# Eight sequences without a loop, score units in two halves, and a step order by priorities

## The reference, cut to what matters

```python
x = x + causal_attention(layernorm(x), Wq, Wk, Wv, Wo)      # 16 heads of 16, rotary, causal
x = x + routed(layernorm(x), Wg, Wq, Wk, Wv, Wo)            # half of the tokens by gate, 16 heads of 16
x = x + biased_attention(layernorm(x), w_qkv, w_out, bias)  # 16 heads of 64, relative bias
x = x + routed(layernorm(x), Wg, Wq, Wk, Wv, Wo)
```

## Time and profile before

| | us |
|---|---|
| median of three runs | 2933.91 (2921.36 to 2938.8) |
| profiled execution | 2932.05 |
| its span, first to last instruction | 2930.3 |
| TensorE busy | 2390.6 (82%) |
| VectorE, ScalarE, GpSimd busy | 1303.9, 1131.5, 533.8 |
| DMA | 98.24 MB, 34 GB/s |

### The profile page before, as it was taken

The page is one execution under the profiler, slowest core; times in us unless marked ns, Lnnn a source line. Parts: engine busy times, 40 slices in busy tenths (PEclk is TensorE's granted clock), DMA queues, the critical chain, the costliest instruction groups (busy, mean ns, idle before and its releaser), DMA issues. The chain is left out here.

```text
span 2930.3 us, 38346 instructions
## 1 busy us (share of the span) xinstructions
PE 2390.6 (82%) x15600; PEld 1367.1 (47%) x15616; DVE 1303.9 (44%) x3344; ACT 1131.5 (39%) x1873; POOL 533.8 (18%) x755
## 2 busy tenths in 40 slices
PE   5578888887888888788788878888878888888996
PEld 3344455443455444554345543554435544355554
DVE  3345453453434445444354354544435444354433
ACT  2234442444424344244442434424444234443551
POOL 2102221121201222012220122101221112211220
PEclk8889999999999899999999989999999998999998
DMA  2001110110001110011100101001010010001100
GB/s 97 1 18 43 37 37 19 37 51 24 31 19 37 51 37 31 7 44 44 37 31 11 51 31 37 31 23 41 31 37 31 24 47 28 31 31 42 55 21 8
DMA packets 28919, 98.24 MB, mean 34 GB/s; under 512 B 2752, under 2 KB 11328, under 8 KB 28608
## 3 DMA queue, kind: packets, MB, share of 16 engines
q1 hardware_dynamic: 28736, 95.70, 9.7%
HBM read 91.49 MB, written 4.19 MB: 33 GB/s over the span
## 5 line engine op out<-in xcount | busy, mean ns | idle before, releaser
L641 ACT ACTIVATE probs<-probs,peak 128x512 f32<-128x512 f32 x512 | 365.2, 714 | 608.9 <-DVE peak L819 608.7
L577 POOL TENSOR_SCALAR probs<-probs,rtotal 128x512 f32<-128x512 f32 x512 | 354.6, 706 | 1221.6 <-DVE rtotal L823 1221.6
L813 DVE CUSTOM_DVE_ANT_0 probs<-ps,band 128x512 f32<-128x512 f32 x512 | 332.1, 686 | 397.1 <-PE ps L1057 397.1
L648 ACT ACTIVATE PT<-ps 128x1024 f32<-128x1024 f32 x256 | 259.9, 1016 | 168.4 <-PE ps L1064 167.8
L1057 PE MATMUL ps<-KT,QT 64*128 64x512 f32 x1024 | 299.3, 662 | 10.7 <-ACT PT L648 3.9
L729 DVE TENSOR_REDUCE mcol<-ps 128x4 f32<-128x512 f32 (+3 forms) x128 | 187.8, 1490 | 242.3 <-PE ps L901 242.3
L1064 PE MATMUL ps<-ident,probs 128*128 128x128 f32 x2048 | 279.6, 281 | 7.4 <-ACT PTc L606 3.8
L484 PE MATMUL ps<-xnT,wb 128*128 128x512 f32 x512 | 273.1, 663 | 14.1 <-ACT xnT L593 8.9
L1064 PEld LDWEIGHTS ps<-ident,probs 128*128 128x128 f32 x2048 | 235.0, 144 | 90.6 <-issue 77.1
L1071 PE MATMUL ps<-PT,Vb 128*64 128x512 f32 x1024 | 254.8, 643 | 3.7 <-ACT PT L648 3.7
L606 ACT ACTIVATE PTc<-ps 128x1536 f32<-128x1536 f32 (+1 forms) x96 | 152.5, 1589 | 147.2 <-PE ps L914 146.8
(11 more groups left out here) (125 smaller groups left out, 3124.4 us busy)
## 6 DMA issues: line engine op xcount, KB each, us to landing
band<-in_band SPq DMA_DIRECT2D x64, 896.0 KB, 4.6
wb<-in_w_b SPq DMA_DIRECT2D x64, 384.0 KB, 3.0
x<-in_x SPq DMA_DIRECT2D x8, 512.0 KB, 4.0
out<-x SPq DMA_DIRECT2D x16, 256.0 KB, 2.2
wob<-in_wo_b SPq DMA_DIRECT2D x1, 1024.0 KB, 7.0
wqk<-in_wqk_a SPq DMA_DIRECT2D x1, 512.0 KB, 4.5
wva<-in_wv_a SPq DMA_DIRECT2D x1, 256.0 KB, 4.1
woa<-in_wo_a SPq DMA_DIRECT2D x1, 256.0 KB, 4.2
```

The source lines that it names most:

```text
L577: last = g.tensor_scalar(unit, unit, rtotal[:, r % 8, e:e + 1], 1.0, ALU.mult, ALU.mult)
L641: last = a.activation(unit, unit, ACT.Exp, bias=peak[:, r % 8, e:e + 1], accum_out=total[:, r % 8, e:e + 1])
L648: a.activation(PT[:, k % 2, :, :, tile_of(q)], bank(now).rearrange("p e (k n) -> p e k n", k=NT), ACT.Copy).then_inc(act_read, 1)
L813: last = v.tensor_tensor_reduce(out=probs[:, r % ROWS_HELD, e, :], in0=bank(now)[:, e, :], in1=band[:, k % 2, e, lo:lo + T], scale=1.0, sc ...
```

## The change

The three lists of steps now name for each step what it needs and what it must follow; `whole` joins the parts of all eight sequences, and `in_order` makes the order. It simulates the engines with the durations of `WORK` (in us; the first entry is where a step begins) and takes, again and again, the step with the smallest `key`: the time at which it could start (inputs, banks, 0.1 us for another tile shape, 0.15 us for a signal), less the allowance of its kind in `EARLY`; no start counts as earlier than TensorE's next free moment. Ties go to the step with the longest chain of needs behind it. A biased part's first steps may come before the last rows of the one before. By the table, the 99 TensorE steps of a biased part add up to 145 us (`b_q` and `b_k` 1.75, `b_v` 1.85, `b_xt` .95, others below), and the allowances of one sequence's side steps and biased transposes to 96 us.

Each `c_p1`, `c_p2`, `f_p1`, `f_p2` has two units of two banks, `o` for heads 0 and 1 and `o2` for heads 2 and 3, anywhere in PSUM. TensorE waits for room in both, and raises the first unit's signal after the last matmul of head 1. The reader waits and reads twice. `f_p1` and `f_p2` are changed as `c_p1` and `c_p2` are. There is one program for all steps, without loop or barriers between; what was cleared by them counts on (`16 * (k // 2 + 1)` and the like), and waits for the first loads stand where the data is first used.

```diff
 UNITS = {
...
-    "c_p1": [("o", "dve", 4)], "c_m": [("o", "dve", 1)], "c_p2": [("o", "act", 4)], "c_val": [("o", "act", 1)],
+    "c_p1": [("o", "dve", 2), ("o2", "dve", 2)], "c_m": [("o", "dve", 1)],
+    "c_p2": [("o", "act", 2), ("o2", "act", 2)], "c_val": [("o", "act", 1)],
...
-    "f_p1": [("o", "dve", 4)], "f_m": [("o", "dve", 1)], "f_p2": [("o", "act", 4)], "f_val": [("o", "act", 1)],
+    "f_p1": [("o", "dve", 2), ("o2", "dve", 2)], "f_m": [("o", "dve", 1)], "f_p2": [("o", "act", 2), ("o2", "act", 2)],
+    "f_val": [("o", "act", 1)],
...
+WORK = {
+    "c_ln": [("dve", 2.4), ("pool", 1.6), ("dve", 1.8)],
+    "c_xt": [("pe", .95), ("act", 1.1)],
...
+    "f_gate": [("dve", .35)],
+    "f_row": [("pe", .5), ("dve", 3.8)],
+    "f_rank": [("pe", 1.9), ("dve", 3.1)],
+    "f_gather": [("pe", 3.5), ("act", .6)],
...
+    "f_p1": [("pe", .95), ("dve", 1.24), ("dve", 1.24)],
+    "f_m": [("pe", .3), ("dve", .4)],
+    "f_p2": [("pe", .95), ("act", 1.03), ("act", 1.03)],
...
+    "b_row": [("pe", .95), ("dve", 1.75), ("act", 1.85)],
+    "b_nrm": [("dve", .17), ("pool", 1.4)],
+    "b_tr": [("pe", .9), ("act", 1.05)],
+    "b_val": [("pe", 3.55), ("dve", .7)],
+    "b_y": [("pe", 6.95), ("dve", 2.1)],
+    ("c_p1", 0): [("pe", 1.15), ("dve", .97), ("dve", .97)],
...
+TILES = {"c_p2": 1, "f_p1": 1, "f_p2": 1, "b_row": 2, "c_val": 3, "f_val": 3, "b_val": 4}
+CHANGE, SIGNAL = 0.1, 0.15
+
+EARLY = {
+    "b_k": -0.5, "b_ln": 0.25, "b_v": -0.57, "b_xt": 2.17, "b_y": 0.44, "c_ln": 0.15, "c_m": 0.5, "c_ot": 1.06,
+    "c_p1": 0.5, "c_p2": 2.06, "c_qk": 1.11, "c_rot": 0.64, "c_t1": 0.5, "c_turn_k": 0.5, "c_turn_q": 0.5,
+    "c_v": 0.89, "c_val": 0.5, "c_xt": 0.67, "c_y": 0.77, "f_gate": 1.71, "f_gather": 1.51, "f_k": 0.54, "f_ln": 0.69,
+    "f_m": 0.65, "f_o": 0.25, "f_p1": 0.61, "f_p2": 1.25, "f_q": 0.35, "f_rank": 1.28, "f_row": 0.53, "f_t1": 0.53,
+    "f_v": 0.74, "f_val": 0.73, "f_y": 0.65,
 }
...
+STORE_LOAD, FETCH = 6.5, 4.6
...
+    for g in range(4):
         for u in range(3):
...
+            out.append((c("p1", g, u), [c("turn_q", g // 2), c("turn_k", g // 2)],
+                        ([c("m", g - 2)] if g >= 2 else []) + ([c("p1", g, u - 1)] if u else [])))
+            out.append((c("p2", g, u), [c("m", g)],
+                        ([c("val", g - 1, u)] if g else [c("v", 1)]) + ([c("p2", g, u - 1)] if u else [])))
+            out.append((c("val", g, u), [c("p2", g, u), c("v", 1)], [c("val", g, u - 1)] if u else
+                        [c("val", g - 1, 2)] if g else []))
+        out.append((c("m", g), [c("p1", g, 2)], []))
+    for i in range(2):
...
+def whole():
+
+
+    steps = []
+
+    def add(layer, needs, follows):
+        first, a, b = layer[0]
+        steps.extend([(first, a + needs, b + follows)] + layer[1:])
+        return [layer[-1][0]]
+
+    entered = add(causal_steps(0), [], [])
+    side = entered = add(ffn_steps(0, 1), entered, [])
+    for s in range(B):
+        biased = add(biased_steps(s, s - 1 if s else None), entered, [])
+        gone = []
+        if s > 0:
+            side = gone = add(ffn_steps(s - 1, 3), left, side)
+        if s + 1 < B:
+            side = add(causal_steps(s + 1), gone, side)
+            side = entered = add(ffn_steps(s + 1, 1), side, [])
+        left = biased
+    add(ffn_steps(B - 1, 3), left, side)
+    return steps
...
+def in_order(steps):
+
+
+    known = {x for x, _, _ in steps}
+    work = {x: WORK[x.kind if x.kind in WORK else (x.kind, x.q)] for x in known}
+    needs = {x: [(y, SIGNAL + (STORE_LOAD if x.kind == "c_ln" else FETCH if x.kind == y.kind == "b_row" else 0))
...
+    def spot(banks):
+        return min(range(0, BANKS, banks), key=lambda b: (max(bank_free[b:b + banks]), max(bank_used[b:b + banks])))
+
+    while ready:
+        best = None
+        for x in ready:
+            if xn_held and x.kind in ("c_ln", "f_ln", "b_ln"):
+                continue
+            engine = work[x][0][0]
+            start = max([free[engine]] + [done[y] + wait for y, wait in needs[x]])
+            if engine == "pe":
+                if TILES.get(x.kind, 0) != tiles:
+                    start += CHANGE
+                if x.kind != "c_val" or x.q == 0:
+                    units = UNITS[x.kind]
+                    banks = units[0][2]
+                    start = max(start, sorted(max(bank_free[b:b + banks]) for b in range(0, BANKS, banks))[len(units) - 1])
+            key = (max(start, free["pe"] + 0.1) - EARLY.get(x.kind, 0), -chain[x])
+            if best is None or key < best[0]:
+                best = key, x, start
+        _, x, t = best
+        ready.remove(x)
+        emptied = {"act": [], "dve": []}
+        for i, (engine, us) in enumerate(work[x]):
+            t = max(t + (SIGNAL if i else 0), free[engine]) + us
+            free[engine] = t
+            if i and engine != "pool":
+                emptied[engine].append(t)
+        if work[x][0][0] == "pe":
+            tiles = TILES.get(x.kind, 0) if x.kind != "c_p1" else 0
+        done[x] = t
+        for i, (name, reader, banks) in enumerate(UNITS.get(x.kind, ())):
+            opened = x._replace(q=0) if x.kind == "c_val" else x
+            at = banks_of[x, name] = banks_of[opened, name] if opened in done and opened != x else spot(banks)
+            for b in range(at, at + banks):
+                bank_free[b] = emptied[reader][min(i, len(emptied[reader]) - 1)] + SIGNAL
+                if x.kind == "c_val" and x.q < 2:
+                    bank_free[b] = 1e9
+                bank_used[b] = len(order)
+        if x.kind in ("c_ln", "f_ln", "b_ln"):
+            xn_held = True
+        if x.kind in ("c_xt", "b_xt", "f_gather"):
+            xn_held = False
+        order.append(x)
...
-                            pool.wait_ge(act_read, plan.unit(now, now))
+                            pool.wait_ge(act_read, plan.unit(now, now, "o2"))
...
                         if kind == "c_p1":
                             e = n % 2
-                            for t, o, w in c_p1_parts(q):
-                                last = v.tensor_reduce(max_places(mcol[:, e, t, :], e), bank(now)[:, :, o:o + w],
-                                                       AXIS.X, ALU.max)
-                            last.then_inc(dve_read, 1)
+                            for i, name in enumerate(("o", "o2")):
+                                dve.wait_ge(dve_full, plan.unit(now, now, name))
+                                for t, o, w in c_p1_parts(q):
+                                    last = v.tensor_reduce(max_places(mcol[:, e, t, :], e)[:, 2 * i:2 * i + 2],
+                                                           bank(now, name)[:, :, o:o + w], AXIS.X, ALU.max)
+                                last.then_inc(dve_read, 1)
...
                             read(now, Step("c_turn_q", s, l, c))
                             read(now, Step("c_turn_k", s, l, c))
                             room(now)
+                            room(now, "o2")
+                            o = head_banks(now)
                             parts = c_p1_parts(q)
                             for i, (t, at_, w) in enumerate(parts):
                                 for h in range(4):
-                                    te.matmul(o[:, h, at_:at_ + w], Qz[group(h), c, e, tile_of(t)], K1[group(h), c, e, 0:w],
+                                    te.matmul(o[h][:, at_:at_ + w], Qz[group(h), c, e, tile_of(t)], K1[group(h), c, e, 0:w],
                                               start=(i == 0), stop=False)
                             for i, (t, at_, w) in enumerate(parts):
                                 for h in range(4):
-                                    last = te.matmul(o[:, h, at_ + w - P:at_ + w], identb[:], later[:], start=False,
+                                    last = te.matmul(o[h][:, at_ + w - P:at_ + w], identb[:], later[:], start=False,
                                                      stop=(i == len(parts) - 1))
+                                    if i == len(parts) - 1 and h == 1:
+                                        full(last, now)
+                            full(last, now, "o2")
+                            continue
...
-            nc.all_engine_barrier(sems_to_clear=stretch_sems)
...
-        stretch(causal_steps(0), {}, {}, False)
-        with nc.Block() as loaded:
-            @loaded.sync
-            def _(sp):
-                sp.wait_ge(w_rest, 6 * 16)
-                sp.wait_ge(b_first, 5 * 16)
-        stretch(ffn_steps(0, 1), {}, {}, False)
-        stretch(stretches([0], False, True, False), {}, {}, True)
-        with nc.Fori(0, B - 3, 2) as it:
-            stretch(stretches([1, 0], True, True, False), {0: it, 1: it + 1}, {0: it + 2, 1: it + 3}, True)
-        stretch(stretches([1], True, False, True), {0: B - 2, 1: B - 1}, {}, False)
+        layers()
```

More of the change, by code:

```diff
@@ L158 @@
-TURN_LAG = 3
-def biased_steps(s):
-    l = 2
[L164 to L185, removed]
@@ L188, in spread, with c @@
```

(34 more changed lines are left out.)

339 lines of the change are left out of this document (192 added, 147 removed).

## The result

The changed kernel takes 2453.4 us in the median of four runs (2451.0 to 2454.8) against 2929.5 of the kernel before in the same comparison: a ratio of 0.837 (0.834 to 0.840). The profiled span is 2450.3 us.

A forecast was written before the change was run, and what follows sets the result against it. TensorE's time (idle, half clock, work) was taken as the bound. Middle 2107.7 / (1 - 0.095 - 0.028) = 2403, head 173, tail 62, sum 2638, with 1.75 around the span 2640 us (-10%); own range 2540 to 2740, over all 2470 to 2850.

The forecast's parts named there:

- What bounds the kernel: Whole kernel: TensorE's time; in the 2671.2 us middle, 434.5 us idle, 129 us clock cost, 2107.7 us full-clock work.
- (a): No loop or barriers: gaps before norms' transposes and VectorE's waits for x shrink, worth 29 to 60 us.
- (b): Split score units: extra reading hides; causal part alone gains 14 us, the lone routed parts 5 and 4 us.
- (c): New order in the middle, biased steps as filler: 28 us idle of some 315 a sequence, 9.5% against 16.3%.
- The clock: Middle: half-clock cost follows the idle share at a ratio of 0.30, so 9.5% idle brings 2.8%.
- dense stretch: Kernel before, 2680 to 2864 us, little side work mixed in: TensorE 3.8% idle at clock 0.99, taken as a bound.
- the 2107.7 us of work stay: Middle: matmuls keep their number and shape, so full-clock work remains 2107.7 us.
- Dense: Rival, middle: biased steps fill everything, idle 3.8%, clock cost 1.1%, 2453 us in all; chance 0.17.
- The side chain ends last: Rival: routed, causal, routed parts in sequence delay the next biased part; 335 to 358 us a sequence, 2695 to 2833; chance 0.18.
- Little is gained: Rival: readers' delays cause idle time whatever the order; only barriers and x waits go, 2890 us; chance 0.09.
- Allowances used in full: Rival, TensorE's queue before side steps: all 96 us a sequence is waited, 3155 us, slower; chance 0.09.
- Bunched transposes: Rival, biased rows' transposes: 421 ns in place of 273 for 2048, adding 303 us, 2943 us; chance 0.01.

The follow-up runs named there:

- unroll: The kernel before's order and four-bank units, written out for all eight sequences without loop and barriers; 2884.9 us, ratio 0.986 against the kernel before.
- serial: The change, but the next biased part's norm may start only when the last biased part's output is added; 2595.6 us, 0.885 of the kernel before.
- early2: The change with all allowances in `EARLY` doubled; 2694.3 us, 0.918 of the kernel before.
- four_same: The change's very order of steps with four-bank units, only the split undone; 2550.3 us, 0.871 of the kernel before.
- early0: The change with all allowances in `EARLY` set to zero; 2967.1 us, 1.012 of the kernel before.
- early01: The change with all allowances in `EARLY` at a tenth; 2670.1 us, 0.910 of the kernel before.
- order_only: The new order planned for four-bank units, no loop, no split, biased transposes also following the second last b_v; 2596.4 us, 0.887 of the kernel before.
- row_twice: The change with each biased row's two matmuls issued twice into the same banks, same order of steps; 2631.0 us, 0.897 of the kernel before.
- tuned_b: The change with other simulation constants, allowances found anew, biased norm's transposes also behind the second last b_v; 2436.0 us against the change's 2450.8.
- early2b: The change with allowances doubled and each biased norm's transposes also behind the two b_v steps before the last; 2725.4 us, 0.929 of the kernel before.

## Why the prediction was wrong, step by step

**What bounds the kernel** was right: TensorE's time, made of idle time, clock and work, and idle time that an order with biased filler can take away.

**(a)** "Worth 29 at least, 60 at most" held by the number: *unroll* gained 35. Its mechanism held only in part. The waits before norms' transposes fell by 16 us and not by 29, and VectorE's wait for x stayed at 29.1 of 31.2 us. It is the new order that took it away; this is the changed kernel:

```profile
L755 DVE BATCH_NORM_STATS2 stats<-x 128x6 f32<-128x256 f32 x128 | 48.1, 418 | 11.8 <-PEq L1210 10.2
```

What was not priced there is the overlap of two biased parts, which only the new order uses and which *serial* puts at 145 us.

**(b)** Duration and count of the halves were right and hidden. The gain of the parts that run alone was sized too small: causal part 91.4 us (forecast 100), routed 58.4 (60), tail 61 (62): 211 us after the loads where the sum had 222. And the split was priced only for these lone parts. In the middle I let it come under (c); it is worth 100 to 112 us over the kernel. The bank waits that I read were those for other score units; the 45.7 us behind biased units were left out.

**(c)** is the step that failed: "28 us of some 315, and with a little from the biased part itself 9.5% idle" (the terms as listed make 29). It was 18.3 us of 294 (294.33 - 276.02), 6.2%. I took each allowance as a wait that happens. For the score units that was near: second scores waited 3.6 us in the causal part and 4.2 in the routed ones, where 3.6 and 4.8 were counted, and first causal scores 2.8 us for banks, where the count had 4. The others hardly came: the norms' transposes were given 2.8 us a sequence, the first projection 1.1 and the turn-backs 2.1, and none of these waits in the steady period; for row, rank and gather it was 6.6, and 1.9 came. As I read the key, an allowance only bites where the step's input is nearly there and nothing else is; a long reader (3.8 us for the ranks) is bridged by biased rows first. No run tests this reading by itself.

**The clock** was mis-sized too: "a ratio of 0.30" between clock cost and idle share. It was 0.28 before, with the windows in the right place, and here 6.3% idle brought 0.4%, a ratio of 0.06. The dense stretch's 0.99 was a rounded figure for 184 us, and the 0.30 came from an order with 43 gaps of over 2 us (135 us in all); the change has none behind its first transposes.

The middle's miss of 177 us (2403 against 2226) so divides into idle time 228 - 139 = 89, clock 67 - 8 = 59, and 29 us of work; the parts run alone make up the other 11. The work was "the 2107.7 us of work stay". The clock windows had made that figure too small (2114.1 is right), and it did not stay: 2078.7. The kernels with the old list have 2114 to 2119, those with the new way of ordering 2068 to 2093. By the lists, TensorE changes tile shape 1120 times in the old order and 881 times in the new one, which the simulation charges for; 0.16 us each would do. But *early2* has only 716 changes and 2069.8 us, 9 us less than the change where that price would make it 26, and *four_same*, with the same list as the change, has 2070.3. So the price is not borne out. Why there is less work stays open.

**The rivals.** *Dense* (0.17) is what came, by its number, and that was luck in part: idle time is 6.3% and not 3.8, clock cost 0.4% and not 1.1, work 2079 us and not 2108, and the lone parts are 11 us shorter. These errors cancel. *The side chain ends last* was well seen as a mechanism, since *early0* and *early01* are just that, but the change's priorities avert it; my queueing price of 113 us a chain was 275 - (58.4 + 91.4 + 58.4) = 67. *Little is gained* is ruled out by *order_only* (2596.4); *unroll*'s 2884.9 against its 2890 is what loop and barriers give alone. *Allowances used in full* did not come at the change's values: doubling them costs 275 us and still leaves the kernel faster than before, and the one that came out longer than before has none. *Bunched transposes* did not lose the clock: they keep a median of 273 ns, as in the earlier trace rows:

```profile
L1194 PE MATMUL ps<-ident,probs x2048: 272/273/473, 260.0 to 2369.4; 128*128 128x128 f32 x187
```

## What to carry to other kernels

Where one engine is the bound and its queue is in order, place a step when its inputs are ready, and measure the idle time by asking what could have stood in that place: here the list alone was worth 322 to 335 us, loop and barriers 35. Give the dependent chain priority over the filler, even with a wait of a microsecond, because the filler runs out if the chain that opens the next batch of it comes late (*early0*, *early01*). Keep bank units small: one that needs four neighbouring banks waits for every small unit that another step holds among them.

## What was not expected of the hardware

The idle share alone doesn't set the clock's cost. *early0* is idle for 16.8% of its middle and loses 6.5% to half clock; *early01* is idle for 11.8% and loses 2.8%; *early2* is idle for more, 14.0%, and loses only 1.8%. Part of it is how the idle time is bunched. The two first have the stretches of side work alone, as in the windows above (clock 0.82 and 0.80), while the same kernels ran at 1.00 on both sides of them. The kernels whose middle has no gap of over 2 us behind the first transposes (the change, *four_same*, *row_twice*, *tuned_b*) lose 0.2 to 1.0%. In the change the gaps are 1.4 us at most, and it ran at half clock for 20.5 of 2226 us.

Long gaps are not all of it. *early2b* has the idle share of *early2* and as many gaps of over 2 us (31, with 77 and 76 us in all), and loses 3.1% where *early2* loses 1.8%. What sets the two apart no run here shows.
